# Four split edge rows of twenty in every sweep of a three-layer graph attention kernel, in place of five, five and six

## The reference

```python
z = (x @ W).reshape(N, num_heads, head_dim)
e = leaky_relu(el[src] + er[dst], 0.2)      # el, er: sums of z * attn_l, z * attn_r
ex = exp(e - segment_max(e, dst)[dst])
alpha = ex / segment_sum(ex, dst)[dst]
out = segment_sum(alpha[:, :, None] * z[src], dst) + z + bias
```

## Time and profile before

| what | value |
|---|---|
| median of 3 runs | 2788.51 us |
| profiled execution, its own time | 2792.58 us |
| its span in the trace | 2790.9 us |
| mean granted TensorE clock | 0.967 |
| PE busy | 2546.9 us (91%) |
| DVE busy | 2158.4 us (77%) |
| ACT busy | 1242.0 us (45%) |
| POOL busy | 1488.1 us (53%) |
| gathers (L677) | 945 + 300, 943.6 + 294.9 us |
| matmuls of L1065 on `parts` | 1332 records, 332.3 us |

### The profile page before, as it was taken

One profiled execution on the slowest core, in us unless ns is written; L12 is line 12 of the kernel. 1 busy time (PEld: TensorE's weight loads), 2 busy tenths in 40 slices (PEclk: granted clock), 3 DMA queues, 4 the chain that ended last, 5 costly groups with the idle time before them and its releaser, 6 DMA issues.

```text
span 2790.9 us, 53062 instructions
## 1 busy us (share of the span) xinstructions
PE 2546.9 (91%) x13226; PEld 1800.2 (65%) x13229; DVE 2158.4 (77%) x4457; ACT 1242.0 (45%) x2607; POOL 1488.1 (53%) x1528
## 2 busy tenths in 40 slices
PE   2997999999999979999999999799999998679998
PEld 1886666666668866666666688556565555467776
DVE  6776999999997769999999977577776776853332
ACT  1223666666654435666666544233333335511111
POOL 1003777777722147777777312477777772124443
PEclk9998999999999989999999999899999999879999
DMA  6445999999958889999999687899999999967776
GB/s 213 165 169 198 336 345 348 339 340 331 333 202 211 216 215 326 346 342 335 345 345 337 216 221 210 231 334 333 337 325 338 334 340 342 358 131 145 145 146 117
DMA packets 199342, 763.41 MB, mean 274 GB/s; under 512 B 41889, under 2 KB 58033, under 8 KB 198542
## 3 DMA queue, kind: packets, MB, share of 16 engines
q0 software_dynamic: 127632, 604.14, 66.3%
q1 hardware_dynamic: 53790, 108.21, 12.8%
q10 hardware_dynamic: 17760, 48.79, 4.4%
HBM read 640.01 MB, written 133.45 MB: 277 GB/s over the span
## 4 chain that ended last, share of the span: by engine, by line
PE 51%; DVE 21%; issue 8%; DMA 7%; POOL 6%; ACT 4%; SPq 2%; ACTq 1%; DVEq 1%; POOLq 0%
PE PS L1065 28%; DVE arena L1512 6%; PE PS L984 6%; PE PS L1188 5%; POOL arena L677 4%; PE PS L1177 4%; DMA arena<-table,src_k 4%; PE PS L986 3%; DVE parts L1530 2%; SPq L498 2%; PE PS L1161 1%; DVE arena L1349 1%; DVE arena L1381 1%; DVE arena L1371 1%; DVE arena L1370 1%
## 5 line engine op out<-in xcount | busy, mean ns | idle before, releaser
L677 POOL DMA_INDIRECT arena<-table,src_k x945 | 943.6, 998 | 309.1 <-issue 191.0
L1065 PE MATMUL PS<-arena,S 128*128 128x384 f32 (+1 forms) x1848 | 676.3, 500 | 4.6 <-DVE arena L1512 4.6
L1512 DVE TENSOR_TENSOR arena<-arena,PS 128x768 f32<-128x768 f32 x630 | 580.8, 947 | 0.9 <-ACT arena L827 0.9
L1065 PEld LDWEIGHTS PS<-arena,S 128*128 128x128 f32 x1848 | 341.8, 191 | 180.6 <-issue 14.5
L1065 PE MATMUL PS<-parts,S 128*128 128x384 f32 (+2 forms) x1332 | 332.3, 371 | 54.1 <-DVE parts L1530 28.7
L677 POOL DMA_INDIRECT W<-table,src_k x300 | 294.9, 983 | 92.6 <-issue 74.6
L623 POOL DMA_DIRECT2D table<-arena x75 | 41.5, 554 | 564.5 <-DVEq L1393 388.3
L1065 PE MATMUL PS<-arena,S_weighted 128*128 128x384 f32 (+1 forms) x840 | 307.7, 508 | 18.1 <-DVE S_weighted L1518 18.1
L1065 PEld LDWEIGHTS PS<-parts,S 128*128 128x128 f32 x1332 | 221.5, 189 | 97.2 <-issue 84.3
L835 ACT ACTIVATE apart<-iota_row,dst_k 128x128 f32<-128x128 f32 x830 | 260.3, 389 | 19.7 <-issue 9.1
L786 ACT ACTIVATE parts<-arena 128x780 fp32r<-128x780 f32 x168 | 142.6, 851 | 248.4 <-DVE arena L1512 240.5
(11 more groups left out here) (295 smaller groups left out, 4530.2 us busy)
## 6 DMA issues: line engine op xcount, KB each, us to landing
arena<-mixed SPq DMA_DIRECT2D x63, 384.0 KB, 3.6
table<-arena POOLq DMA_DIRECT2D x50, 396.0 KB, 3.2
local_b<-local SPq DMA_DIRECT2D x123, 160.0 KB
mixed<-sums ACTq DMA_DIRECT2D x50, 384.0 KB
arena<-table SPq DMA_DIRECT2D x50, 384.0 KB, 4.7
arena<-table,src_k POOLq DMA_INDIRECT x945, 5.7
table<-arena POOLq DMA_DIRECT2D x25, 384.5 KB, 4.6
out<-last_bias POOLq DMA_DIRECT2D x25, 384.0 KB, 6.3
```

Source lines behind the costliest of these rows:

```text
L677: nc.gpsimd.indirect_dma_start(edge_row(l, k % U)[:, 0:table_width(l)], None, table[l][:, :], bass.IndirectOffsetOnAxis(src_k[:, k:k + 1]. ...
L1065: o = nc.tensor.matmul(flat[:, bass.ds(bank + 512 * c, n)], onehot, row[:, c * HALF:c * HALF + n], start=False, stop=True, skip_group_chec ...
L1512: nc.vector.tensor_tensor(z, z, a, ALU.mult).then_inc(s_msg, 1)
```

## The change

```diff
-SPLIT = ((2, 7, 10, 12, 17), (2, 7, 10, 12, 17), (1, 4, 7, 11, 14, 17))
+SPLIT = ((2, 7, 12, 17), (2, 7, 12, 17), (2, 7, 12, 17))
```

## The result

The changed kernel takes 2768.45 us (median of 4 runs, 2764.62 to 2771.63) against 2788.32: a ratio of 0.9929, 95% interval 0.9912 to 0.9947, 20 us less. The forecast was 2781.0 with a range of 2771 to 2796. The direction held; the gain was more than twice the 7.5 us forecast, and the time lies 2.5 us under the range. Its profiled execution took 2764.62 us, with a span of 2762.9.

A forecast was written before the change was run, and what follows sets the result against it. It took DVE's round to bound the first two sweeps and POOL's gather issuing the third; -7.0 - 1.8 + 1.3 = -7.5 us from 2788.51 gave 2781.0, range 2771 to 2796.

The forecast's parts named there:

- -7.0 forecast: First sweep: 546.6 us new (538.0 of groups, 5.6 start, 3.0 waits) against 553.6; ends -10 and +6.
- 3 us for what remains of waits: First sweep: of PE's 23.7 us of waits after the start, 3 would be left.
- -1.8 forecast: Second sweep: 550.0 us new against 551.8, with 9.0 more for the start and 3 for waits; ends -5 and +4.
- In both sweeps the bound goes over from DVE to PE: First two sweeps: PE's round of 26.00 us would set the pace, -0.30 a round in the first, +0.12 in the second.
- PE can come at most 5 us nearer: Second sweep: limit on PE's end nearing the last gather, from 21.4 us behind there against 16.4 in the third.
- +1.3 forecast: Third sweep: PE's new work hides under POOL's pace and only the end shows, +1.3 us; ends -4 and +12.
- ACT and DVE lose 42 leading copies and rests, neither is full, nothing follows: Third sweep: 42 fewer leading copies and rests on ACT and DVE would change no time.
- 20 or more: Third sweep: sign of a right forecast, PE's idle time falling by 20 us or more.
- rival (a): Fewer rests quicken gathers, up to 6 us in the third sweep, 4 in the second; 7 taken, 2774 us; chance 0.15.
- (b): Third sweep: PE falls behind bursts of gathers and holds POOL up, +11 in total, 2800 us; chance 0.10.
- (d): All three sweeps: nothing covers PE's added work, +54.6 us, 2843; chance 0.02.
- (c): First two sweeps: the waits stay, 0 to +6 us in each, total about +5, 2793 us; chance 0.21.

The follow-up runs named there:

- five_place_11: The changed kernel with splits at (2, 7, 11, 12, 17) in the first two sweeps and (2, 12) in the third; ratio 0.9983 to the kernel before.
- three_everywhere: The changed kernel with three splits, at (2, 7, 12), in all sweeps; ratio 1.0004 to the kernel before.
- six_late_places: The changed kernel with six splits in the third sweep, at (2, 4, 7, 12, 14, 17); ratio 0.9953 to the kernel before.
- four_early_places: The changed kernel with the third sweep's four splits at (1, 7, 11, 17); ratio 0.9936 to the kernel before.
- more_dve_sbuf: The changed kernel plus 332 unused VectorE instructions behind the third sweep's rests, both operands in SBUF; ratio 1.0017 to the kernel before.
- more_dve_psum: The changed kernel plus 332 unused VectorE instructions behind the third sweep's rests, one operand in SBUF, one in PSUM; ratio 0.9953 to the kernel before.
- before_rest_whole: The kernel before with each first-sweep rest done in one VectorE instruction instead of two around a message; ratio 1.0055 to the kernel before.
- third_only: The kernel before with only the third sweep changed, to splits at (2, 7, 12, 17); 2785.0 us, ratio 0.9998.
- first_two: The kernel before with only the first two sweeps changed, to splits at (2, 7, 12, 17); 2771.1 us, ratio 0.9944.

## Why the prediction was right and wrong

**First sweep, -7.0 forecast, -8.9 measured.** The mechanism was right: DVE's round of 26.30 gives way to PE's of 26.00 (`five_place_11` keeps DVE's, `three_everywhere` lengthens PE's). The start stayed (row 7 comes 14.9, 15.0 us after row 0 before and 15.4, 13.4 after). Mis-sized is the term "3 us for what remains of waits": in the trace after, 545.2 less 538.0 and a start of 6.1 (15.4 - 9.3) leaves 1.1.

**Second sweep, -1.8 forecast, -3.4 measured,** inside its ends, but the mechanism was wrong in part. "In both sweeps the bound goes over from DVE to PE" doesn't hold here: DVE's round of 25.88 was already under PE's 26.00, and what paced the sweep as a whole were the gathers, held up for only 1.8 us in all. They took 1.317 us each, 26.3 a round, and 1.297 after, with the excess beside rests down from 21.3 to 13.2 us. Only so did PE's 26.00 become the bound. "PE can come at most 5 us nearer" took the gathers' pace as fixed: from first to last they are 8.1 us shorter (537.0 for 545.1), and PE ends no nearer behind the last (23.1 us, before 21.3). The start of this sweep, which I took from one trace, scatters (row 7 after 18.3 and 16.6 us before, 16.7 and 17.2 after).

**Third sweep, +1.3 forecast, -4.5 measured.** This is the step that failed: "ACT and DVE lose 42 leading copies and rests, neither is full, nothing follows". POOL was rightly named as the bound, and PE's new work was indeed hidden. PE's shortest round went from 23.57 to 24.79 us, some 25 us a sweep; its busy time rose by 13 us only and its idle time fell by 17, from 34 to 17 us, not by the 20 or more that I had named as a sign. But I took POOL's pace as its own. It depends on what DVE does beside it: `six_late_places` against `four_early_places`, and `more_dve_sbuf` against `more_dve_psum`, show it, and so does the excess beside rests, 11.6 us before and 7.4 after. I had that as rival (a) with 0.15, on one row, and set it aside because the median gather was untouched. The median is the wrong figure; the mean over the median was 17.9 us in that sweep, and it went to 397.2 - 405 x 0.947 = 13.7. Over all traces the gathers' step went from 1.295 to 1.285 us, which is 4.3 us in 414 steps, beside the 4.5 measured.

**Between the sweeps, 0 forecast, -4.5 measured.** The sum has no term for it, and that is the second step that failed. DVE, now ahead of PE when a sweep ends, has the next layer's first rows ready sooner, so PE's first transposes start 2.03 us after its last product in place of 4.40. DVE's last message of the first sweep ended 6.9 us before PE's last product, where it was 4.6, and the transposes start 8.95 us behind that message in 12 of the 14 traces (9.35 in `before_rest_whole` and `three_everywhere`), so it is DVE's lead that moves them. The time from the first to the second sweep follows the split count of the first (216.4 to 216.9 with place 10, 215.6 with five and place 11, 213.4 to 215.3 with four splits, 212.7 with three); no experiment was made on this step alone. The transposes themselves are shorter as well in this pair of traces (0.85 for 1.51 us), but that isn't DVE's lead: in `third_only` they take 0.85 after an idle time of 4.59.

```profile
820.85 0.85 PE L969 MATMUL PS<-ident,arena 128*128 128x128 f32 x6 [4.59 <-issue]
```

**The rivals.** (b) and (d) are out: POOL never waited for PE in the third sweep (the gap is 0.30 before each gather in the traces of both kernels), and PE's 26 us there were not seen. (c) is out by `first_two`, whose first two sweeps have rounds of 26.00 with hardly a wait. (a) was the nearest, at 2774, and its "up to 6" and "up to 4" us were of the right size.

The range ended at 2771, with rival (a) and a little more. The three sweeps together, -16.8, would have come to 2771.7, just inside it; the 4.5 us between them, for which no step allowed, took the time out of it.

## What to carry to other kernels

Where two engines are both full, moving work from one to the other pays until their rounds are equal, and the rounds can be read from the distance of one instruction to itself a round later; here PE's new one was forecast to 0.01 us. An engine that never waits is a bound, but its speed need not be its own: look at the mean of its instructions over their median, and at what the others do beside the long ones. A median round can mislead as well: in the second sweep of before DVE's said 25.88 us, while POOL, held up for 1.8 us in all, needed 26.3 on average. And when the bound goes over from an engine that feeds to the one that is fed, count the ends of the loop too, for the feeder then arrives early at whatever comes next.

## What the runs showed of the hardware that was not expected

332 VectorE instructions of 0.38 us with both tiles in SBUF added 27 us to the time of 405 gathers that GpSimd issued beside them; the same with one tile in PSUM added 4.3 us, and 0.1 us to the 80 gathers that had nothing but them beside it. Doing a subtraction of 780 columns in one instruction of 0.96 us behind a message, in place of two of 0.56 around it, five times a round, added 25 us to GpSimd's time in the first sweep. The same six transposes of PE behind a sweep took 1.51 us in some traces and 0.85 in others; the idle time ahead of them doesn't decide it (1.51 after 4.40 us and 1.52 after 2.81, 0.85 after 2.03 and 4.59), and the cause is open.
